# Half the queries of four heads at a time: a new split of scores, exponentials and values in an attention and mixture-of-experts kernel

## The reference, cut to what matters

```python
h = layernorm(x) * (1 + ca) + sa                        # x: 8 batches, 512 tokens, 128 wide
q = (h @ Wq.T).reshape(B, S, 16, 8).transpose(0, 2, 1, 3)   # 16 heads of 8
k, v = h @ Wk.T, h @ Wv.T                               # one key and value head for all
dist = softmax(einsum('bhqd,bkd->bhqk', q, k) / sqrt(8))
x = x + ga * einsum('bhqk,bkd->bhqd', dist, v)          # heads side by side
h = layernorm(x) * (1 + cb) + sb
x = x + gb * top2_of_8_experts(h)                       # router, gelu MLPs, weighted sum
```

## Time and profile before

| | |
|---|---|
| median of 3 runs | 648.71 us (648.13 to 651.44) |
| span of the profiled execution, first to last instruction | 616.6 us |
| what lies around the span (median less span; the profiled execution's own whole time isn't listed) | 32.1 us |
| PE, DVE, ACT, POOL busy in the span | 554.9, 496.7, 443.5, 320.6 us |
| attention loop (67 to 448 us) | 381 us, 32 groups |
| granted TensorE clock, mean | 0.977 |

### The profile page before, as it was taken

How to read it: one execution, slowest core, us unless ns; L and a number is a source line. 1 busy time by engine, 2 the same in 40 slices (tenths; PEclk the granted TensorE clock), 3 DMA queues, 4 the chain that set the end, 5 groups by cost and what they waited for, 6 DMA issues and landing times.

```text
span 616.6 us, 18921 instructions
## 1 busy us (share of the span) xinstructions
PE 554.9 (90%) x6699; PEld 307.3 (50%) x6699; DVE 496.7 (81%) x1134; ACT 443.5 (72%) x776; POOL 320.6 (52%) x574
## 2 busy tenths in 40 slices
PE   3669999999999999999999999999799999899970
PEld 2222334333443443443343343343289998799970
DVE  5887999898789779789789779888667777656687
ACT  5683588888788778778877877878765555367771
POOL 1623010134456656666667566666326757665670
PEclk9989999999999999999999999999899999899995
DMA  6299400310311220220220140001223223232645
GB/s 190 66 282 343 132 10 10 75 37 8 78 30 29 69 58 21 70 65 18 61 79 16 35 105 17 27 20 29 51 62 95 79 79 100 84 90 65 201 138 175
DMA packets 49868, 49.32 MB, mean 80 GB/s; under 512 B 15616, under 2 KB 44336, under 8 KB 49056
## 3 DMA queue, kind: packets, MB, share of 16 engines
q1 hardware_dynamic: 42256, 36.89, 21.8%
q0 software_dynamic: 4320, 9.38, 4.7%
q10 hardware_dynamic: 3200, 1.84, 1.0%
HBM read 29.40 MB, written 17.10 MB: 75 GB/s over the span
## 4 chain that ended last, share of the span: by engine, by line
PE 66%; DVE 17%; ACT 5%; issue 3%; DMA 3%; POOL 2%; SPq 2%; DVEq 0%; ACTq 0%; POOLq 0%
PE ps L1096 15%; PE ps L1055 14%; PE ps L1086 12%; DVE neg_max L1401 10%; PE ps L1164 10%; PE ps L1175 9%; ACT P L1263 3%; ACT diag L1273 2%; PE ps L1123 1%; DMA k_parts<-parts 1%; PE ps L1138 1%; PE ps L1155 1%; PE ps L1074 1%; POOL h_sorted L810 1%; PE ps L1130 1%
## 5 line engine op out<-in xcount | busy, mean ns | idle before, releaser
L1401 DVE TENSOR_REDUCE neg_max<-ps 128x1 f32<-128x512 f32 x512 | 321.1, 684 | 54.5 <-PE ps L1055 52.2
L1263 ACT ACTIVATE P<-ps,zero 128x1024 f32<-128x1024 f32 x256 | 272.0, 1110 | 72.8 <-PE ps L1086 71.0
L1055 PE MATMUL ps<-K,Q 128*32 128x512 bf16 x2048 | 183.3, 383 | 5.5 <-DVE neg_max L1401 5.1
L1086 PE MATMUL ps<-Q,K 128*32 128x512 bf16 x2048 | 155.9, 381 | 5.5 <-ACT P L1263 5.1
L1096 PE MATMUL ps<-P,V 128*32 128x512 f32 x1024 | 134.1, 598 | 1.2 <-ACT P L1263 1.1
L1055 PEld LDWEIGHTS ps<-K,Q 128*32 128x32 bf16 x2048 | 54.5, 96 | 109.3 <-DVE neg_max L1401 59.8
L1613 POOL DMA_INDIRECT y_rows<-P,to_now x71 | 73.9, 1041 | 62.9 <-DVE P L1453 30.7
L1319 ACT ACTIVATE parts<-ps,parts 128x128 f32<-128x128 f32 x228 | 64.9, 370 | 41.8 <-PE ps L1164 39.5
L1086 PEld LDWEIGHTS ps<-Q,K 128*32 128x32 bf16 x2048 | 52.3, 97 | 75.7 <-issue 29.5
L810 POOL DMA_INDIRECT h_sorted<-diag,slot x64 | 64.7, 1010 | 28.6 <-POOL max_parts L79 13.4
L1164 PE MATMUL ps<-parts 128*128 128x128 f32 x456 | 61.6, 279 | 2.7 <-DVE parts L1441 1.3
(11 more groups left out here) (239 smaller groups left out, 576.5 us busy)
## 6 DMA issues: line engine op xcount, KB each, us to landing
Q<-q_parts SPq DMA_DIRECT2D x24, 384.0 KB
xs<-h_sorted SPq DMA_DIRECT2D x71, 72.0 KB
W<-w_t SPq DMA_DIRECT2D x2, 2048.0 KB, 11.2
q_parts<-parts SPq DMA_DIRECT2D x8, 384.0 KB, 3.5
Q<-y_rows SPq DMA_DIRECT2D x6, 512.0 KB, 4.5
diag<-att_u SPq DMA_DIRECT2D x128, 16.0 KB
Q<-max_parts SPq DMA_DIRECT2D x96, 4.0 KB, 1.9
out<-Q SPq DMA_DIRECT2D x6, 256.0 KB, 2.3
```

What stands on the lines that cost most here:

```text
L1055: ins = eng.matmul(ring_bank(*unit)[QUAD * q:QUAD * (q + 1), :], Q[buffer_of(g)][:, g % NG * G + j, at:at + QUAD], K[buffer_of(g)][:, 0, : ...
L1086: ins = eng.matmul(bank(2 * u + j)[QUAD * q:QUAD * (q + 1), :], K[p][:, 1, at:at + QUAD], Q[p][:, g % NG * G + 2 * u + j, :], start=True, ...
L1263: nc.scalar.activation(P[s % 2][:, 2 * u:2 * u + 2, :], bank(2 * u, 2).rearrange("p (j t) -> p j t", j=2), ACT.Exp, bias=zero[:], scale=SC ...
L1401: eng.tensor_reduce(neg_max[g % 2][:, j * T + s:j * T + s + 1], ring_bank("maximum", g, s, j), AX.X, ALU.max, negate=True).then_inc(ring_u ...
```

## The change: what it does

A `scores` call no longer takes two heads with all 512 queries, but all four heads with 256 queries: bank `2u + j` holds heads `2j` and `2j + 1` for half `u` of the queries. The matmuls are as many and as wide (512 columns, now two stretches of 256). An exponential reads two banks as before and writes four stretches of 256 into `P`. Half of the queries is then complete for all four heads, so `values` is called per half: four fp32 matmuls of 256 columns. The first half's values of the step before go behind the second M of a step, the second half's behind the fourth. `pv_done` now counts halves. In a group's first step both halves of the last step stay together in the old place.

```diff
                     for j in range(2):
+                        first = g % NG * G + 2 * j
                         for q in range(128 // QUAD):
                             at = 128 * s + QUAD * q
-                            ins = eng.matmul(bank(2 * u + j)[QUAD * q:QUAD * (q + 1), :], K[p][:, 1, at:at + QUAD],
-                                             Q[p][:, g % NG * G + 2 * u + j, :], start=True, stop=True, tile_position=(0, QUAD * q))
+                            to = bank(2 * u + j)[QUAD * q:QUAD * (q + 1), :].rearrange("p (j t) -> p j t", j=2)
+                            ins = eng.matmul(to, K[p][:, 1, at:at + QUAD], Q[p][:, first:first + 2, some], start=True, stop=True,
+                                             tile_position=(0, QUAD * q))
...
-                def values(g, s):
-
-                    if s == 0 and g > 0:
+                def values(g, s, u):
+
+                    some = slice(HALF * u, HALF * (u + 1))
+                    if s == 0 and u == 0 and g > 0:
                         eng.wait_ge(att_out, START + g)
-                    eng.wait_ge(exp_done, START + (g * T + s) * 2 + 2)
+                    eng.wait_ge(exp_done, START + (g * T + s) * 2 + u + 1)
                     for j in range(G):
-                        ins = eng.matmul(bank(7)[QUAD * j:QUAD * (j + 1), :], V[buffer_of(g)][:, s, :], P[s % 2][:, j, :],
-                                         start=(s == 0), stop=(s == T - 1), tile_position=(0, QUAD * j))
+                        ins = eng.matmul(bank(7)[QUAD * j:QUAD * (j + 1), some], V[buffer_of(g)][:, s, :], P[s % 2][:, j, some],
+                                         start=(s == 0 and u == 0), stop=(s == T - 1 and u == 1), tile_position=(0, QUAD * j))
...
-                            if s > 0 and j == G - 1:
-                                values(g, s - 1)
+                            if s > 0 and j % 2 == 1:
+                                values(g, s - 1, j // 2)
                             if s == 0 and j == 1 and g > 0:
-                                values(g - 1, T - 1)
+                                values(g - 1, T - 1, 0)
+                                values(g - 1, T - 1, 1)
...
-                    if u == 0 and g * T + s >= 2:
-                        eng.wait_ge(pv_done, START + g * T + s - 1)
-                    eng.wait_ge(score_done, START + (g * T + s) * 2 + u + 1)
-                    nc.scalar.activation(P[s % 2][:, 2 * u:2 * u + 2, :], bank(2 * u, 2).rearrange("p (j t) -> p j t", j=2),
+                    n = g * T + s
+                    if n >= 2:
+                        eng.wait_ge(pv_done, START + (n - 2) * 2 + u + 1)
+                    eng.wait_ge(score_done, START + n * 2 + u + 1)
+                    nc.scalar.activation(P[s % 2][:, :, HALF * u:HALF * (u + 1)], bank(2 * u, 2).rearrange("p (j t) -> p j t", j=G),
                                          ACT.Exp, bias=zero[:], scale=SCALE).then_inc(exp_done, 1)
```

More of the change, by code:

```diff
@@ L608, in adaln_block @@
         late_loaded = [sem(f"late_loaded{n}") for n in range(PIECES)]
-        LAST = B - 1
+        LAST, HALF = B - 1, S // 2
         def buffer_of(g):
@@ L1012, in _ @@
                     if refill:
-                        eng.wait_ge(pv_done, START + g * T)
+                        eng.wait_ge(pv_done, START + g * T * 2)
                         load_operands(eng, b, b % 2, batch_loaded, 0, 1)
@@ L1076, in scores @@
                 def scores(g, s, u):
-                    p = buffer_of(g)
+                    p, some = buffer_of(g), slice(HALF * u, HALF * (u + 1))
                     if s == 0 and u == 0:
@@ L1210, in _ @@
                                 ranks(batch_at(g, 5))
-                            if s > 0 and j == G - 1:
-                                values(g, s - 1)
+                            if s > 0 and j % 2 == 1:
+                                values(g, s - 1, j // 2)
                             if s == 0 and j == 1 and g > 0:
-                                values(g - 1, T - 1)
+                                values(g - 1, T - 1, 0)
+                                values(g - 1, T - 1, 1)
                             if s == 0 and j == 1 and g + 1 < GROUPS:
                                 turn_maxima(g + 1)
-                values(GROUPS - 1, T - 1)
+                for u in range(2):
+                    values(GROUPS - 1, T - 1, u)
                 eng.wait_ge(experts_loaded, START + 4 * 16)
@@ L1252, in out_of_bank @@
                 def out_of_bank(g):
-                    eng.wait_ge(pv_done, START + (g + 1) * T)
+                    eng.wait_ge(pv_done, START + (g + 1) * T * 2)
                     if g >= 2:
```

## The result

The changed kernel takes 645.11 us (median of 8 runs, 642.68 to 646.20) against 650.64 for the kernel before in the same comparison (8 runs, 646.16 to 653.55): a ratio of 0.9938, interval 0.9909 to 0.9967. Repeated beside other kernels it was 0.9934 (0.9910 to 0.9957). So it is faster, by 4 us and not by the 9.6 forecast. The time lies within the range that I gave, near its slow end, which I had put there for the rivals and not for what happened; so that is luck.

The account below looks back on a forecast made before the run. PE's own stream was taken to set the pace, leaving only its waits to win. Order -10.35, half passes +0.6 and the later ranks' copy +0.15 gave -9.6: 648.7 to 639.1 us, range 634.5 to 646.

Parts of the forecast that it names:

- a batch saves 1.65: Loop batch: groups with heads and ranks save 0.43 us, statistics 0.36, normalization 0.43, logits 0.43; six such batches ahead of group 29.
- signs of being wrong: In the loop: half passes over 0.22 us apart, exponentials over 1.15 us, or PE waiting for DVE as long as before.
- Scores and exponentials at nothing: Loop's scores and exponentials: operand in two stretches, output in four, taken as free, exponentials staying at 1,110 ns.
- A half pass at 0.216: Loop's values: each 256-column quad pass costs 0.216 us, about +2 ns on each of 256 added passes, +0.6 us.
- a fixed price per added matmul: Rival, loop's values: each 256-column record costs more than its half; 651 us at 0.24 us per half pass; chance 0.06.
- Waits form anew: Rival, loop groups: later second scores and exponentials and a busy DVE bring 0.3 us of new waits each; 648 us; chance 0.10.
- The array's queue can't deliver: Rival, PE in the loop: 96 records per step at 27 ns can't be kept up; 703 us at 32 ns; chance 0.06.
- The order: Loop steps: first half of values moves ahead of the third maximum, so PE waits shrink; 10.35 us saved in all.
- The loop's end at 0: Groups 29 to 31 and after: ranks' copy to row transpose stays 19.9 us; afterwards 0, bounds -0.5 to +2 us.
- The experts' part untouched: Experts' part, outside the loop: the change does not touch it, so no time was added or saved there.
- 616.6 + 32.1: Whole kernel: profiled execution's span of 616.6 us plus 32.1 us around it, the median by construction, as base of the forecast.

## Why the prediction was wrong, point by point

**The step that failed is "a batch saves 1.65", counted six times.** It was read from a batch of the earlier trace rows in which the scatters cost nothing, and I took this for how the kernel runs; the scatters stand at nothing in the sum. Without scatters each part of it is right: heads and ranks -0.41 (forecast -0.43), statistics -0.42 (-0.36), normalization -0.42 (-0.43), logits -0.38 (-0.43), together 48.71 to 47.07. Over the intervals 11 to 30 that is 8.1 us. With scatters 4.6 us are left, since the scatters cost 12.1 us instead of 8.6. Two of the signs of being wrong that I had named did not show: half passes start 0.216 apart, not over 0.22, and exponentials take 1,113 ns, not over 1,150. Of a batch, heads and ranks keep their 0.41; statistics and normalization keep 0.3; the logits' interval saves nothing or loses 0.1 (13.07 to 13.15).

**Why scatters cost more now.** The table gives it to the cut: with whole values they cost 8.6, with values in halves 12 to 13, whether one half is moved (12.1) or not (12.8). So the cost comes with cutting the values, and only where there are scatters; without them the cut costs 0.3 us over twenty intervals. That it goes by the number of records isn't shown: a quarter of the added records less gave nothing back behind scatters. What it is there that makes halves worse was not shown either. One reading is that PE lives on what stands queued for it while no semaphore moves, and that a queue of given length holds half as much time in halves. Two things speak against it. The pair with more scatters, where it should have shown again, grew alike in both kernels. And in the stretches of the intervals 11 to 30 PE goes on starting matmuls for 0.37 us on average in the kernel before, for 0.42 with the values cut in place and for 0.49 in the changed kernel, so it isn't seen to run dry sooner. This stays open.

**A wait that I did not foresee: +0.85 us.** Interval 5. The scores of group 5 wait for the transfer of its maxima, which SP issues behind the first refill and the regrouping. It appears in all kernels with every value cut (11.70 to 12.52), with scatters and without. It is neither in the kernel before (11.13) nor in the changed one with whole values in a group's first step (11.09). The transfer isn't issued later; it takes longer, and in every such trace a packet of instruction loading runs beside it, as told above. That this is the cause is argued, not tested.

**Scores and exponentials at nothing:** right (1.0007, exponentials 1,113 ns). **A half pass at 0.216:** right, 0.215 to 0.216 in plain stretches. The rival "a fixed price per added matmul" is refuted there: the 32 added records of a plain group cost 0.02 us in all. "Waits form anew" named the time that came nearest in the end (648), but not the reason: its 0.3 us in every group, from DVE's lag, is missing without scatters, where each kind of group saves what was forecast. The Trainium skill, "TensorEngine Tiling (Array Packing)", section Instruction Overhead, by whose 60 cycles I had estimated +25.6 us, is not borne out as an added cost for four matmuls side by side; by the section's own example, in which a matmul of one column takes as long as one of 60, it is rather a floor, which 256 columns exceed. **"The array's queue can't deliver":** refuted as told, since steps without the long passes run at 27 ns per record; cutting in place was slower all the same, by 8 us, through the scatters.

**The order:** right in its mechanism and its size. From the first transpose of maxima to the last values, the kernel cut in place takes 391.8 us without scatters and the changed kernel 381.5: 10.3 us for the order, where the forecast had 10.35. With scatters the times show 15 us between both halves late and one half early.

**The loop's end at 0:** within its bounds. From the last transpose of maxima to the last values it takes 24.4 us instead of 23.6, 21.5 instead of 20.0 without scatters. The chain of the earlier trace rows is as long in both kernels to 0.3 us, as forecast, but not 19.9 us: from the ranks' copy to the row transpose it takes 22.1 us before and 21.8 after, and 19.2 and 18.6 without scatters. **The experts' part untouched:** its instructions, yes; its time perhaps not. In profiles of the kernel before and of the four made from it that keep the scatters it takes 189.0 to 190.2 us, at a mean granted clock of 0.907 to 0.918; in the two of the changed kernel 191.2 and 191.9 us, at 0.902 and 0.909, and in the four made from that one 189.4 to 192.5 us, at 0.926 to 0.894. So 1 to 2 us of the loop's gain may be lost there; no run tests why. The short execution of the earlier trace rows is left out of this, with its 169 us.

**The sum.** From the first transpose of maxima to the last values, the loop took 401.8 us before and 396.6 after: -5.3. Without scatters it took 389.7 and 381.5: -8.3, which is the forecast of -9.6 with the new wait taken off (-8.8) and 0.5 more. By times that pair differs by 7.6 us of medians, or 5.7 by the ratios of each to its own runs of before, with some 4 us of uncertainty either way. The timed runs of the change itself say -4, with an interval from -2.1 to -5.9 that holds the loop's -5.3. Of these -5.3, the intervals 0 to 10 give -1.5, with the new wait in them, the intervals 11 to 30 give -4.6, and the loop's end takes 0.8 back.

**The absolute time.** 616.6 + 32.1 was no fixed frame: what lies around the span is 1.8 us, and the other 30 were time that this execution did not spend, 8.6 of it in the loop behind scatters, 1.2 at the loop's end and 20 in the experts' part, which scatters throughout. The trace could not show this, but span and median side by side could have: 32 us with no engine at work should have been asked about before a saving was read off that trace.

## What to carry to other kernels

Where the span of a profiled execution and the median of the timed ones stand further apart than another profile of a like kernel explains, the trace is of another situation; a gain read from it counts only for the part of the program that runs alike in both. When a transfer holds up every engine at once, leave it out in both kernels: here that alone split the answer, 8.3 us of gain without scatters and 5.3 with. A cut that costs 0.02 us in a quiet group cost 4.2 us behind the scatters of twenty groups, so a cut should be timed by itself in the part with the worst neighbours; and the early place needed the cut, since whole values there cost 27 us.

## What was unexpected of the hardware

Around a pair of indirect scatters of 128 rows each, issued by POOL, semaphore updates of all engines come to a halt two to five times, mostly for 0.45 to 0.7 us: ACT took up scores 1.5 us after they were complete, and DVE restarted in the same hundredth of a microsecond as ACT. The loop's scatters cost 8.6 us over the intervals 11 to 30 in the kernel before and 12.1 in the changed one, though POOL is busy for only 31.5 us in a batch of 50. In one of the two profiled executions of the kernel before, the same scatters cost nothing (48.71 us per batch, as without them). What differed in that execution is not known.

Where a packet of 16 KB that loads instructions ran beside the transfer of group 5's maxima, for 1.2 to 1.4 us, PE's scores waited for that transfer; it landed 9.7 to 10.5 us into the interval, where it otherwise did at 8.5 to 8.9.
